# Experts on 32 tiles of 256 tokens and 7 of 128 instead of 39 of 256, with another routing chain and products of zeros beside it

## Chip, cores and metric

The kernel runs on one core of one Trainium2 chip. The metric is the device time of one execution in microseconds, from the first to the last instruction and the little around it; the median of three executions stands for a kernel.

## The reference

The input is one sequence of 4096 tokens with 256 features. Three parts follow one another, each on the layer norm of the residual stream: a mixture of experts (half its output is added), a causal attention with 16 heads, and the same mixture of experts again.

```python
logits = einsum('bsd,de->bse', x, gate_w) + gate_b
probs = softmax(logits, axis=1)                 # over the tokens
vals, idx = top_k(probs, 2)                     # 2 of 8 experts for each token
h = relu(einsum('bsd,edo->ebso', x, w1) + b1)   # three layers of 256 x 256
h = relu(einsum('ebso,eop->ebsp', h, w2) + b2)
y = relu(einsum('ebso,eop->ebsp', h, w3) + b3)
v = einsum('ebso,bse->eo', y, w_tok)            # one row of 256 for each expert
out = einsum('bse,eo->bso', ind, v)             # each token adds its two experts' rows
```

Each expert's outputs are summed over its tokens, each weighted by its probability. Only the tokens that chose an expert count, 8192 pairs of token and expert in all.

## The kernel before, in words

Each mixture of experts ("block" f = 0 and f = 1) has a **routing** and a **stream of tiles**. The 8192 pairs are sorted by expert into slots, and each expert's slots are rounded up to whole tiles of 256: at most 39 tiles, whatever the tokens choose, and the kernel always works on 39.

*Routing* (`route`, lines 1291 to 1435 on VectorE) is one chain on VectorE, in which nearly every step waits for the one before (`prev()`); each step counts up the semaphore `routed`, and `ROUTED[name]` is its place. It picks each token's two experts (to `chosen`, L1345), lets TensorE count tokens for each expert (L978, L979), works out where each expert's tiles start (`counts` to `slots`, L1355 to L1378), gives each pair its slot (to `digits_lo`, L1390), and makes one-hot matrices ("hots", L1396 to L1401: four batches of three instructions) from which 64 matmuls (L989) build the inverse, from slot to token. Between the counts and the hots TensorE transposes the chosen experts for the later combination (L985, eight groups of four matmuls, which ScalarE copies out at L763). From the inverse come the row numbers of each half tile (`code` to `row_no`, L1405 to L1414), then each tile's expert (`tile_cmp` to `tile_mask`) and the matrix that sums tiles to experts (`from_start` to `tile_hot`).

*The stream.* GpSimd gathers a tile's token rows with one indirect DMA for each 128 tokens (`load_tile`, L502), two for a tile, into a ring of three tiles. Then the engines run a software pipeline over j, each in the order that is written out:

- TensorE (`tiles`): third layer of tile j-3, transposes of tile j (L1020, 4), second layer of tile j-2, transposes of its weights (L1027, 2), first layer of tile j-1. A layer (L1009) is 4 products of 128x128 weights with 256 columns in f32; each product is two records in the trace, so a layer has 8 records, and a tile 24 and 6 transposes.
- VectorE (`tiles`): the token weights of tile j (`widen_weight`, L1459 to L1465), bias and weight on the third layer of tile j-3 (`weigh`, L1472), a copy of an expert's layer weights into place (`stage`, L1451, whose expert number is first loaded into a register), bias and relu of the second layer of tile j-2 (`relu_second`, L1481), and two more `stage` copies. The last of the three waits for ScalarE's relu of tile j-1, since it overwrites the bias that this relu reads.
- ScalarE (`tiles`): relu and sum of tile j-3 (L775), the copies of the transposes of tile j (L781, L785), relu of the first layer of tile j-1 (L791).

Activations and staged weights have two buffers each, and each layer has one PSUM bank. After the last tile its sums are transposed (L1042) and combined (L1057) with the residual stream.

## Time and profile before

| what | value |
|---|---|
| median of 3 runs | 2256.11 us (2255.95 to 2260.18) |
| the profiled execution: its own time | 2256.6 us |
| its span | 2254.6 us |
| busy shares: TensorE, VectorE, ScalarE, GpSimd | 95%, 82%, 72%, 23% |
| mean granted TensorE clock | 0.973 |

The profile counts an engine as busy while it executes; loading a register and waiting for a semaphore are not busy time. The granted clock is TensorE's, as a share of 2.4 GHz: 1.00 is 2.4 GHz, 0.50 is 1.2 GHz. Times in the trace are from the start of the span. The stream of block 0 ends at 308.75 us, the attention follows, and block 1 begins its routing at 1960.2 us.

### The profile page before, as it was taken

Reading aid. Unit: us, or ns where it says so; the run is one execution under the profiler, and the core shown is the slowest. Engines: PE = TensorE matmul, PEld = TensorE weight load, DVE = VectorE, ACT = ScalarE, POOL = GpSimd, SP = SyncE. Lnnn points to the kernel's source line nnn. Section 1 sums busy time; section 2 is a strip of 40 time slices with the busy share of each in tenths; the row PEclk is TensorE's granted clock in tenths of the full one; section 3 lists DMA queues with packets and bytes.
Section 4 is the critical chain, followed back from the end, with each engine's and each line's share of the span. In section 5 each row is a group of like instructions: output and inputs, shape, how many; then the busy total and the mean of one; then the engine's idle time right before and its main releaser. Section 6 shows DMA issues by size and latency. Waiting matters only on the chain.

```text
span 2254.6 us, 98008 instructions
## 1 busy us (share of the span) xinstructions
PE 2149.0 (95%) x42449; PEld 1870.9 (83%) x42449; DVE 1850.2 (82%) x3873; ACT 1625.3 (72%) x3556; POOL 528.6 (23%) x1307
## 2 busy tenths in 40 slices
PE   4899988999999999999999999999999999689997
PEld 3788866388999999999999999998999997568885
DVE  7555555899999999999999999999999993765555
ACT  5244445588888888888888888888888887424442
POOL 1333302422121221222212213122122210033330
PEclk8899989999999999999999999999999999879998
DMA  8211203410010110100101001011010002131112
GB/s 262 71 48 47 46 8 102 145 32 17 20 32 4 32 25 11 32 11 25 30 6 32 23 13 32 7 30 25 11 32 12 24 4 93 29 114 48 46 48 81
DMA packets 95527, 96.23 MB, mean 43 GB/s; under 512 B 41332, under 2 KB 84088, under 8 KB 95096
## 3 DMA queue, kind: packets, MB, share of 16 engines
q0 software_dynamic: 42048, 44.80, 7.9%
q1 hardware_dynamic: 52624, 45.15, 6.3%
q8 instruction: 334, 5.47, 1.0%
q14 instruction: 97, 0.79, 0.1%
q10 hardware_dynamic: 424, 0.01, 0.0%
HBM read 64.14 MB, written 25.43 MB: 40 GB/s over the span
## 4 chain that ended last, share of the span: by engine, by line
PE 89%; DVE 4%; issue 3%; ACT 1%; POOL 1%; DMA 1%; SPq 1%; ACTq 0%; POOLq 0%; DVEq 0%
PE bank L1108 43%; PE bank L1100 19%; PE bank L1009 18%; PE bank L1146 2%; PE bank L1020 2%; PE bank L1063 1%; PE bank L1211 1%; PE bank L989 1%; DVE stats L1241 1%; PE bank L1027 1%; PE bank L1154 1%; PE bank L1076 0%; SPq L621 0%; DVE rows L1263 0%; DVE x_res L1514 0%
## 5 line engine op out<-in xcount | busy, mean ns | idle before, releaser
L1108 PE MATMUL bank<-work 96*32 96x512 bf16 (+4 forms) x17920 | 1413.2, 363 | 3.2 <-DVE work L1553 2.8
L842 ACT ACTIVATE feat<-bank 128x512 f32<-128x512 f32 (+3 forms) x2304 | 1251.5, 565 | 153.9 <-PE bank L1108 76.7
L1553 DVE TENSOR_REDUCE work<-bank 128x1 f32<-128x512 f32 (+3 forms) x2176 | 1299.5, 639 | 62.0 <-PE bank L1108 50.3
L1100 PE MATMUL bank<-feat,phase 128*17 128x128 f32 x16896 | 1137.8, 272 | 1.6 <-issue 1.6
L1100 PEld LDWEIGHTS bank<-feat,phase 128*17 128x17 f32 x16896 | 829.5, 98 | 66.9 <-issue 2.5
L1108 PEld LDWEIGHTS bank<-work 96*32 96x32 bf16 (+1 forms) x17920 | 808.1, 96 | 69.3 <-DVE work L1553 11.4
L1009 PE MATMUL bank<-work 128*128 128x256 f32 x1872 | 434.9, 382 | 3.7 <-issue 2.6
L1009 PEld LDWEIGHTS bank<-work 128*128 128x128 f32 x1872 | 340.6, 191 | 53.9 <-issue 12.3
L1451 DVE COPY work<-phase 128x514 f32 x234 | 100.5, 429 | 189.5 <-DVE work L1472 56.4
L560 POOL TENSOR_SCALAR_AFFINE_SELECT feat<-feat 128x128 f32<-128x128 f32 x512 | 147.2, 295 | 444.5 <-ACT feat L842 436.2
L502 POOL DMA_INDIRECT work<-token_table,row_no x156 | 149.2, 956 | 327.6 <-DVE work L1465 242.0
L775 ACT ACTIVATE work<-work 128x256 f32<-128x256 f32 x156 | 63.6, 408 | 180.9 <-DVE work L1472 180.9
L791 ACT ACTIVATE work<-bank,work 128x256 f32<-128x256 f32 x156 | 65.5, 471 | 87.5 <-PE bank L1009 79.3
L567 POOL TENSOR_TENSOR rows<-work 128x64 f32<-128x64 f32 x128 | 37.5, 293 | 330.4 <-DVE work L1564 306.2
L529 POOL DMA_DIRECT2D work<-qk_parts x180 | 107.0, 596 | 5.1 <-PE bank L1108 3.2
L551 POOL CAST work<-work 128x4 bf16<-128x4 f32 x128 | 24.0, 187 | 340.2 <-DVE work L1559 340.2
L1550 DVE TENSOR_REDUCE work<-bank 128x4 f32<-128x512 f32 x128 | 88.0, 688 | 1.6 <-PE bank L1154 1.6
L1146 PE MATMUL bank<-work 96*32 96x128 bf16 (+3 forms) x2048 | 84.4, 201 | 0.8 <-issue 0.8
L1472 DVE SCALAR_TENSOR_TENSOR work<-bank,work 128x256 f32<-128x256 f32 x156 | 67.8, 475 | 11.1 <-PE bank L1009 10.9
L1146 PEld LDWEIGHTS bank<-work 96*32 96x32 bf16 x2048 | 68.7, 95 | 9.8 <-issue 3.3
L781 ACT ACTIVATE work<-bank 128x512 f32<-128x512 f32 x78 | 45.0, 577 | 42.6 <-PE bank L1020 40.7
L1108 PE MATMUL bank<-ident,work 128*32 128x68 f32 x1024 | 70.7, 226 | 0.4 <-ACT work L858 0.4
(175 smaller groups left out, 1414.0 us busy)
## 6 DMA issues: line engine op xcount, KB each, us to landing
phase<-in_w SPq DMA_DIRECT2D x12, 1024.0 KB, 11.7
work<-qk_parts POOLq DMA_DIRECT2D x60, 192.0 KB, 4.2
token_table<-rows SPq DMA_DIRECT2D x8, 1056.0 KB, 9.6
qk_parts<-phase SPq DMA_DIRECT2D x20, 384.0 KB, 2.7
work<-qk_parts POOLq DMA_DIRECT2D x60, 128.0 KB, 4.3
qk_parts<-work SPq DMA_DIRECT2D x12, 384.0 KB, 2.6
x_res<-in_x SPq DMA_DIRECT2D x8, 512.0 KB, 8.8
work<-work SPq DMA_DIRECT2D x256, 1.0 KB
```

The lines of the kernel that those rows point to most:

```text
L502: eng.indirect_dma_start(out=x_slot[:, j % NXG, u, :], out_offset=None, in_=table[f], in_offset=bass.IndirectOffsetOnAxis(ap=row_no[:, n:n ...
L529: eng.dma_start(stack[r * HD:(r + count) * HD, h % 2, c, tokens], src).then_inc(sig.stack[h % 2], 16)
L560: eng.affine_select(out=p_ring[:, n % P_RING, lo:lo + P], in_=p_ring[:, n % P_RING, lo:lo + P], compare_op=ALU.is_ge, fill=0.0, base=0, pa ...
L842: eng.activation(p_ring[:, n % P_RING, lo:QB], s_bank("probs", n)[:, lo:QB], ACT.Exp, scale=HD ** -0.5).then_inc(sig.s_done, 1)
L1009: mm = eng.matmul(bank[bk][:, m * TILE:(m + 1) * TILE], staged[:, b, l, k * D + m * P:k * D + (m + 1) * P], acts[:, l, b, k], start=(k == ...
L1100: mm = eng.matmul(bank[ACC_BANK][GRID * g:GRID * g + VW, 0:P], v_aug[:, t, h, :], p_ring[:, n % P_RING, g * P:(g + 1) * P], start=(t == 0) ...
L1108: mm = eng.matmul(out[GRID * g:GRID * (g + 1), width], left[:, GRID * g:GRID * (g + 1)], right, start=start, stop=stop)
L1146: eng.matmul(tiles[GRID * g:GRID * (g + 1), i, 0:GRID * (g + 1)], stack[0:QK_ROWS, h % 2, 0, q0 + GRID * g:q0 + GRID * (g + 1)], stack[0:Q ...
L1451: eng.tensor_copy(staged[:, j % 2, l, :], experts[:, bass.ds(expert, 1), l, :].rearrange("p a w -> p (a w)"),).then_inc(sig.staged[f], 1)
L1472: eng.scalar_tensor_tensor(weighted[:, j % 2, m], bank[4][:, m * TILE:(m + 1) * TILE], staged[:, j % 2, 2, KD * D + m:KD * D + m + 1], w_r ...
L1550: eng.tensor_reduce(maxima[:, h % 2, j, :, 0], scores[:, 0:QB].rearrange("p (i s) -> p i s", i=TPJ), AX_X, ALU.max).then_inc(sig.a_done, 1)
L1553: eng.tensor_reduce(maxima[:, h % 2, j, i, k + 1:k + 2], scores[:, 0:hi - lo], AX_X, ALU.max).then_inc(sig.a_done, 1)
```

## The change

The stream has 39 tiles as before, but 32 are wide (256 tokens) and 7 narrow (128 tokens, one gather, products of 128 columns, transposes of half the number). `ORDER` puts a narrow tile first, then five or six wide ones before each further narrow one, and a narrow one last. Where an expert's slots don't fill a wide tile, its rest goes into a wide tile while such are left, and else into one or two narrow ones; the routing chain works this out in new steps on small operands (`rounded` to `beyond_by`), several of which don't wait for the one before. `beyond`, `beyond_slots` and `all_slots` are new on full-size operands. In turn `chosen`, `counts`, `prior`, the tile steps, `code`, `row_f` and `row_clamped` go, the counting matmuls take the operand in the order expert, tile, the inverse is 71 columns wide instead of 78, and the steps from `tile_cmp` to `tile_mask` stand before the wait for the inverse instead of behind the row numbers. Four of the eight groups of L985 move behind the 64 matmuls of L989.

TensorE also multiplies zeros by zeros into bank 4, 512 columns in bf16, with no reader (`busy_beside`): one product after each of the 17 steps before `chosen_bf`, one after each of the 9 steps from `row_scaled`, and 5 more behind them, all of the last 14 ahead of the first tile. In the second step of the stream TensorE does the first layer of tile 0 before the transposes of tile 1.

```diff
-MAGIC = 1.5 * 2 ** 30
-N_TILES = (TOP * S + E * (TILE - 1)) // TILE
-N_SUB = N_TILES * TS
+MAGIC, MAGIC_TILE = 1.5 * 2 ** 30, 1.5 * 2 ** 31
+LO_MIDDLE = (P - 1) / 2
+WIDE, NARROW = TOP * S // TILE, E - 1
+N_TILES = WIDE + NARROW
...
+FIRST_CHOSEN, FIRST_ROW = "chosen_bf", "row_scaled"
+GATHER_FILL = 5
+ORDER = [WIDE]
+for _n in range(NARROW - 1):
+    ORDER += [*range(WIDE * _n // (NARROW - 1), WIDE * (_n + 1) // (NARROW - 1)), WIDE + _n + 1]
+SUBS = [[TS * t, TS * t + 1] if t < WIDE else [WIDE * TS + t - WIDE] for t in ORDER]
...
-                for u in range(TS):
-                    n = j * TS + u
+                for u, n in enumerate(SUBS[j]):
                     eng.indirect_dma_start(
                         out=x_slot[:, j % NXG, u, :], out_offset=None, in_=table[f],
...
-                    ).then_inc(sig.slot[f][j % NXG], 16)
+                    ).then_inc(sig.slot[j % NXG][u], 16)
...
+            def chosen_rows(f, m0, m1):
+                need.wait_ge(sig.chosen_wide[f], 1)
+                need.wait_ge(sig.feat[2 * f], KD * NT // 4)
+                for m in range(m0, m1):
+                    need.wait_ge(sig.chosen_copy[f], m - 1)
+                    for i in range(4 * m, 4 * m + 4):
+                        eng.matmul(bank[m % 2][0:V_ROWS, (i - 4 * m) * P:(i - 4 * m + 1) * P], chosen_wide[:, i, :],
+                                   ident_bf[:, :], start=True, stop=True).then_inc(sig.chosen_tr[f], 1)
+            def busy_beside(f, steps):
+                for name in steps:
+                    need.wait_ge(sig.routed[f], ROUTED[name])
+                    eng.matmul(bank[4][:, :], zeros_bf[:, 0:P], zeros_bf[:, :], start=True, stop=True)
             def route(f):
-                flat = chosen_bf[:, :, :].rearrange("p i e -> p (i e)")
...
+                if f == 1:
+                    need.wait_ge(sig.attended, NT // 2)
+                busy_beside(f, ROUTE[:ROUTE.index(FIRST_CHOSEN)])
...
-                eng.matmul(bank[5][:, 0:NT * E], before[:, :], flat, start=True, stop=True).then_inc(sig.counted[f], 1)
-                eng.matmul(bank[6][:, 0:NT * E], ones_bf[:, :], flat, start=True, stop=True).then_inc(sig.counted[f], 1)
...
+                eng.matmul(bank[5][:, 0:NT * E], not_before[:, :], by_expert, start=True, stop=True).then_inc(sig.counted[f], 1)
+                eng.matmul(bank[6][:, 0:NT * E], ones_bf[:, :], by_expert, start=True, stop=True).then_inc(sig.counted[f], 1)
...
                                start=(b == 0), stop=(b == TOP * NT - 1)).then_inc(sig.inverse[f], 1)
+                chosen_rows(f, NT // 8, NT // 4)
...
+                busy_beside(f, ROUTE[ROUTE.index(FIRST_ROW):])
+                busy_beside(f, ROUTE[-1:] * GATHER_FILL)
                 for j in range(N_TILES + LAYERS):
                     layer(f, j - 3, 2)
+                    if j == 1:
+                        layer(f, j - 1, 0)
                     if j < N_TILES:
                         transpose_tile(f, j)
                     layer(f, j - 2, 1)
                     if j < N_TILES:
                         transpose_weight(f, j)
-                    layer(f, j - 1, 0)
+                    if j != 1:
+                        layer(f, j - 1, 0)
                 need.wait_ge(sig.v_part[f], KD * N_TILES)
...
-                step("chosen", eng.tensor_tensor(chosen[:, :, :], sel[:, 0], sel[:, 1], ALU.add))
...
-                step("chosen_bf", eng.tensor_copy(chosen_bf[:, :, :], chosen[:, :, :]))
...
+                step("chosen_bf", eng.tensor_tensor(chosen_bf[:, :, :], sel[:, 0], sel[:, 1], ALU.add))
+                prev()
+                step("weights", eng.tensor_tensor(rows[:, :, D:ROW], chosen_bf[:, :, :], probs[:, :, :], ALU.mult))
...
                 need.wait_ge(sig.counted[f], 2)
                 prev()
-                step("counts", eng.tensor_copy(em, bank[6][:, 0:NT * E].rearrange("p (i e) -> p e i", e=E)))
...
-                step("running", eng.tensor_tensor_scan(flat_run, carry[:, :, :].rearrange("p e i -> p (e i)"), flat_em,
...
-                step("prior", eng.tensor_tensor(prior, run, em, ALU.subtract))
...
-                step("steps_gt", eng.tensor_tensor(steps_gt[:, :, :], run[:, :, NT - 1:NT].to_broadcast(SE),
...
-                step("tiles_of", eng.tensor_reduce(pe_col(5), steps_gt[:, :, :], AX_X, ALU.add))
...
-                step("tile_end", eng.tensor_tensor_scan(pe_col(6), ones_e[:, :], pe_col(5), 0.0, ALU.mult, ALU.add))
...
-                step("tile_start", eng.tensor_tensor(pe_col(7), pe_col(6), pe_col(5), ALU.subtract))
...
-                step("slot_start", eng.tensor_scalar(pe_col(8), pe_col(7), float(TILE), None, ALU.mult))
...
+                step("running", eng.tensor_tensor_scan(flat_run, carry[:, :, :].rearrange("p e i -> p (e i)"),
+                                                       bank[6][:, 0:NT * E], 0.0, ALU.mult, ALU.add))
+                prev()
+                total, full, rest = run[:, :, NT - 1], pe_col(5), pe_col(9)
+                full_sum, left = small[:, 6, 0:1], small[:, 6, 1:2]
+                step("rounded", eng.tensor_scalar(full, total, (1 - TILE) / 2, MAGIC_TILE, ALU.add, ALU.add))
...
+                step("full", eng.tensor_scalar(full, full, MAGIC_TILE, None, ALU.subtract))
...
+                step("expert_rest", eng.tensor_tensor(rest, total, full, ALU.subtract))
+                step("full_sum", eng.tensor_reduce(full_sum, full, AX_X, ALU.add))
+                prev()
...
+                step("over_half", eng.tensor_scalar(over_half, rest, P + 0.5, None, ALU.is_gt))
+                step("left", eng.tensor_scalar(left, full_sum, -1.0 / TILE, float(WIDE), ALU.mult, ALU.add))
...
+                step("others", eng.scalar_tensor_tensor(others, rest, 0.5, over_half, ALU.is_gt, ALU.subtract))
...
+                prev()
+                step("rank", eng.tensor_tensor_scan(rank, ones_e[:, :], rests, 0.0, ALU.mult, ALU.add))
+                prev()
+                step("in_wide", eng.scalar_tensor_tensor(in_wide, rank, left, rests, ALU.is_le, ALU.mult))
...
+                step("wide_some", eng.scalar_tensor_tensor(wide_some, pe_col(14), float(TILE), full, ALU.mult, ALU.add))
+                step("not_in_wide", eng.tensor_tensor(narrow_of, rests, in_wide, ALU.subtract))
...
+                step("wide_slots", eng.scalar_tensor_tensor(wide_slots, pe_col(15), float(TILE), wide_some, ALU.mult,
+                                                            ALU.add))
+                step("narrow", eng.scalar_tensor_tensor(narrow, pe_col(16), 2.0, pe_col(17), ALU.mult, ALU.add))
...
+                step("wide_end", eng.tensor_tensor_scan(wide_end, ones_e[:, 0:E], wide_slots, 0.0, ALU.mult, ALU.add))
+                step("narrow_sum", eng.tensor_tensor_scan(pe_col(12), ones_e[:, 0:E], narrow, 0.0, ALU.mult, ALU.add))
...
+                step("slot_start", eng.scalar_tensor_tensor(pe_col(8), wide_end, -LO_MIDDLE, wide_slots, ALU.add,
+                                                            ALU.subtract))
+                step("narrow_end", eng.tensor_scalar(narrow_end, pe_col(12), float(P), float(NARROW_0), ALU.mult, ALU.add))
...
+                step("narrow_start", eng.scalar_tensor_tensor(narrow_start, narrow, -float(P), narrow_end, ALU.mult,
+                                                              ALU.add))
+                prev()
+                step("beyond_by", eng.tensor_tensor(beyond_by, narrow_start, wide_end, ALU.subtract))
                 step("position", eng.tensor_tensor(
-                    scratch[:, 3], bank[5][:, 0:NT * E].rearrange("p (i e) -> p i e", e=E),
-                    prior.rearrange("p e i -> p i e"), ALU.add))
...
+                    by_expert(slots), bank[5][:, 0:NT * E].rearrange("p (e i) -> p e i", e=E), run, ALU.add))
...
+                step("beyond", eng.tensor_tensor(beyond, slots, bc(wide_slots, 1, PNE), ALU.is_ge))
...
+                step("beyond_slots", eng.tensor_tensor(beyond, beyond, bc(beyond_by, 1, PNE), ALU.mult))
+                step("slots", eng.tensor_tensor(slots, slots, bc(pe_col(8), 1, PNE), ALU.add))
...
+                step("all_slots", eng.tensor_tensor(slots, slots, beyond, ALU.add))
...
-                step("rounded", eng.tensor_scalar(rounded, slot, 0.5 - P / 2, MAGIC, ALU.add, ALU.add))
...
-                step("digits_hi", eng.tensor_scalar(hi, rounded, MAGIC, None, ALU.subtract))
...
-                step("digits_lo", eng.tensor_tensor(lo, slot, hi, ALU.subtract))
+                step("digits_hi", eng.tensor_scalar(hi, slot, MAGIC, MAGIC, ALU.add, ALU.subtract))
...
+                step("digits_lo", eng.scalar_tensor_tensor(lo, slot, LO_MIDDLE, hi, ALU.add, ALU.subtract))
...
-                need.wait_ge(sig.inverse[f], TOP * NT)
...
-                step("code", eng.tensor_copy(code[:, :], bank[7][:, 0:N_SUB]))
...
-                step("row_f", eng.tensor_copy(row_no_f[:, :], code[:, :].bitcast(I32)))
...
-                step("row_clamped", eng.tensor_scalar(row_no_f[:, :], row_no_f[:, :], 0.0, None, ALU.max))
...
+                step("tile_cmp", eng.tensor_tensor(tile_cmp[:, 0:WIDE, :], bc(tile_slots[:, 0:WIDE], 2, WIDE_E),
...
+                step("narrow_cmp", eng.tensor_tensor(tile_cmp[:, WIDE:N_TILES, :],
...
                 prev()
                 step("tile_mask", eng.tensor_tensor(tile_mask[:, :, :], bc(tile_exp[:, :], 2, TE),
...
+                need.wait_ge(sig.inverse[f], TOP * NT)
+                prev()
+                step("row_scaled", eng.tensor_scalar(row_no_f[:, :], bank[7][:, 0:N_SUB].bitcast(I32), 2.0 ** -16,
+                                                     1.0 - CODE_0, ALU.mult, ALU.add))
+                prev()
+                step("row_no", eng.tensor_scalar(row_no[:, :], row_no_f[:, :], 0.0, None, ALU.max))
...
+                step("first_slot", eng.tensor_tensor(pe_col(7), wide_end, wide_slots, ALU.subtract))
...
+                step("tile_slot", eng.tensor_tensor(slot, tile_col[:, :], narrow_col[:, :], ALU.min))
...
+                step("from_start", eng.tensor_scalar(tile_hot[:, 0, :], pe_col(7), slot, None, ALU.is_le))
+                step("from_end", eng.tensor_scalar(tile_hot[:, 1, :], wide_end, slot, None, ALU.is_le))
...
+                step("start_by", eng.scalar_tensor_tensor(tile_hot[:, 0, :], narrow_start, slot, tile_hot[:, 0, :],
...
+                step("end_by", eng.scalar_tensor_tensor(tile_hot[:, 1, :], narrow_end, slot, tile_hot[:, 1, :],
...
+                need.wait_ge(sig.chosen_tr[f], NT)
+                eng.tensor_tensor(w_pick[:, b, 0:n], x_slot[:, j % NXG, 0:n, D:ROW],
+                                  bc(tile_mask[:, ORDER[j], :], 1, [P, n, E]), ALU.mult).then_inc(sig.w_col[f], 1)
...
+                need.wait_ge(sig.w_tr[f], subs_before(j - 1))
+                eng.tensor_copy(w_wide[:, b, 0:n], bc(w_col[:, b, 0:n], 2, [P, n, P])).then_inc(sig.w_col[f], 1)
...
-                        weighted[:, j % 2, m], bank[4][:, m * TILE:(m + 1) * TILE],
...
+                        weighted[:, j % 2, m, 0:WIDTH[j]], bank[4][:, m * TILE:m * TILE + WIDTH[j]],
...
-                    eng.tensor_scalar(acts[:, 2, j % 2, m], bank[3][:, m * TILE:(m + 1) * TILE],
+                    eng.tensor_scalar(acts[:, 2, j % 2, m, 0:WIDTH[j]], bank[3][:, m * TILE:m * TILE + WIDTH[j]],
```

The same narrowing by `WIDTH[j]` stands in ScalarE's instructions and in `layer`, and the loops over the halves of a tile run over `SUBS[j]`.

## Rows read from the trace of the kernel before

**Rows 1.** The chain that ended last, shares of the span by line.

```profile
PE bank L1108 43%; PE bank L1100 19%; PE bank L1009 18%; PE bank L1146 2%; PE bank L1020 2%; PE bank L1063 1%; PE bank L1211 1%; PE bank L989 1%; DVE stats L1241 1%; PE bank L1027 1%; PE bank L1154 1%; PE bank L1076 0%; SPq L621 0%; DVE rows L1263 0%; DVE x_res L1514 0%
```

**Rows 2.** Windows: length, busy of PE, PEld, DVE, ACT, POOL; clock, DMA, GB/s.

```profile
38.00:55.00 17.00, 5.13 (x34) 3.69 (x34) 14.98 (x35) 10.11 (x12) 0.41 (x1) 0.50 0.60 203
55.00:65.00 10.00, 9.59 (x61) 8.55 (x62) 8.07 (x10) 0.00 (x0) 0.00 (x0) 0.50 0.53 167
76.00:80.00 4.00, 3.42 (x13) 2.57 (x13) 0.43 (x1) 1.24 (x4) 3.08 (x4) 0.71 0.42 113
86.00:299.00 213.00, 212.71 (x1086) 182.85 (x1085) 123.12 (x362) 91.12 (x292) 62.53 (x66) 1.00 0.17 43
```

**Rows 3.** Timeline of one tile of block 1: start, us, instruction, [idle before <-releaser].

```profile
2033.60 0.60 PE L1020 MATMUL bank<-ident,work 128*128 128x128 f32 x4
2034.04 1.89 PE L1009 MATMUL bank<-work 128*128 128x256 f32 x8
2034.09 0.17 DVE L1459 TENSOR_TENSOR work<-work,feat 128x16 f32<-128x16 f32 x1
...
2035.98 3.64 PE L1009 MATMUL bank<-work 128*128 128x256 f32 x16
...
2036.69 0.87 DVE L1481 TENSOR_SCALAR work<-bank,work 128x256 f32<-128x256 f32 x2
...
2037.91 0.84 ACT L791 ACTIVATE work<-bank,work 128x256 f32<-128x256 f32 x2 [1.03 <-PE bank L1009]
...
2039.59 0.43 DVE L1451 COPY work<-phase 128x514 f32 x1 [0.84 <-ACT work L791]
...
2039.94 0.17 DVE L1459 TENSOR_TENSOR work<-work,feat 128x16 f32<-128x16 f32 x1
```

**Rows 4.** Timeline of VectorE, a tile of block 0 that it began late.

```profile
197.57 0.17 DVE L1459 TENSOR_TENSOR work<-work,feat 128x16 f32<-128x16 f32 x1
...
202.71 0.43 DVE L1451 COPY work<-phase 128x514 f32 x1 [0.47 <-issue]
203.05 0.17 DVE L1459 TENSOR_TENSOR work<-work,feat 128x16 f32<-128x16 f32 x1
```

**Rows 5.** Timeline of the weight loads of L933, whose matmuls have 32 columns.

```profile
1957.44 0.53 PEld L933 LDWEIGHTS bank<-ident,v_rest 128*128 128x128 f32 x4
```

**Rows 6.** Timeline of block 0, from the chosen experts to the first tiles.

```profile
45.54 0.29 DVE L1347 CAST chosen_bf<-feat 128x256 bf16<-128x256 f32 x1
...
46.54 0.42 DVE L1355 COPY feat<-bank 128x256 f32<-128x256 f32 x1 [0.24 <-PE bank L979]
...
52.45 1.15 PE L985 MATMUL bank<-ident_bf,work 128*96 128x128 bf16 x8 [0.20 <-ACT feat L763]
52.69 0.81 DVE L1396 TENSOR_TENSOR work<-work,digits 128x1248 bf16<-128x1248 bf16 x1
...
65.75 0.24 DVE L1405 COPY code<-bank 128x78 f32<-128x78 f32 x1 [2.69 <-PE bank L989]
...
66.74 0.20 DVE L1414 CAST row_no<-row_no_f 128x78 uint32<-128x78 f32 x1
...
67.25 1.37 POOL L502 DMA_INDIRECT work<-token_table,row_no  x1 [28.00 <-DVE row_no L1414]
...
68.93 1.04 POOL L502 DMA_INDIRECT work<-token_table,row_no  x1 [0.30 <-issue]
...
71.80 1.11 PE L1020 MATMUL bank<-ident,work 128*128 128x128 f32 x4 [6.08 <-DMA work<-token_table,row_no]
...
79.92 1.97 PE L1009 MATMUL bank<-work 128*128 128x256 f32 x8 [0.58 <-issue]
```

**Rows 7.** Timeline of block 0, the last tiles of the stream.

```profile
293.73 10.53 PE L1009 MATMUL bank<-work 128*128 128x256 f32 x48
...
305.27 1.96 PE L1009 MATMUL bank<-work 128*128 128x256 f32 x8 [1.01 <-issue]
...
308.75 0.41 PE L1042 MATMUL bank<-ident,v_part 128*39 128x128 f32 x2 [1.52 <-ACT work L775]
```

More of the change, by code:

```diff
@@ L190, in attention_steps, with subs_before, slot_uses @@
         yield "divide", u
+def subs_before(j):
+    return sum(len(subs) for subs in SUBS[:max(j, 0)])
+def slot_uses(f, j, u):
+    fills = [n for n in range(j % NXG, N_TILES, NXG) if u < len(SUBS[n])]
+    return f * len(fills) + sum(n <= j for n in fills)
 class Waits:
@@ L753, in route @@
                 widen_ids(f)
[L754 removed]
+                need.wait_ge(sig.routed[f], ROUTED["chosen_bf"])
                 if f == 1:
@@ L1344, in route @@
                 prev()
-                step("chosen", eng.tensor_tensor(chosen[:, :, :], sel[:, 0], sel[:, 1], ALU.add))
+                step("chosen_bf", eng.tensor_tensor(chosen_bf[:, :, :], sel[:, 0], sel[:, 1], ALU.add))
                 prev()
-                step("chosen_bf", eng.tensor_copy(chosen_bf[:, :, :], chosen[:, :, :]))
-                prev()
-                step("weights", eng.tensor_tensor(rows[:, :, D:ROW], chosen[:, :, :], probs[:, :, :], ALU.mult))
-                flat_em, flat_run, flat_prior = (scratch[:, n].rearrange("p i e -> p (i e)") for n in range(3))
```

140 lines of the change are left out of this document (68 added, 72 removed).

## The prediction

> **What bounds the kernel now.** I read the chain of waits first: it names what the end of the span hangs on. By line, nearly all of it is matmuls. L1108 and L1100, 62% of the span, belong to the attention, which the change doesn't touch; L1009, the layers of the expert tiles, holds 18%, and the transposes of the tiles (L1020, L1027) 3% [rows 1]. So the two streams of tiles, some 450 us together, run at TensorE's pace. The windows say the same: from 86 to 299 us TensorE is busy 212.71 of 213.00 us at a granted clock of 1.00. In the routing before it the clock is 0.50: there VectorE is the busy engine, and TensorE works little from 38 to 55 us, then 96% of the time from 55 to 65 us on matmuls of 78 columns without the clock rising; it rises only between 76 and 80 us, once the wide products run [rows 2].
>
> The timeline of one tile tells how much room the other engines have, and that decides what half a tile is worth. From one start of L1459 to the next is 5.85 us [rows 3]. *TensorE:* from the transposes to the second layer are 0.44 us, 0.11 for each of four; from that layer to the next are 1.94 us, which is 8 records and 2 transposes, so 0.216 us a record; 24 x 0.216 + 6 x 0.11 = 5.84 us, so it is never idle. *VectorE:* its busy time alone misleads (123 of 213 us), since loading an expert number is not counted. Its one wait is for ScalarE's relu, which ends at 2037.91 + 0.84 = 2038.75, in front of the last copy; the copy has 0.84 us of non-busy time before it. In a tile that VectorE began late, that time is 0.47 us, and the tile takes 203.05 - 197.57 = 5.48 us [rows 4]. So VectorE needs 5.48 us a tile: 0.37 us of room, no more.
>
> **The narrow tile on TensorE.** A record of 128 columns streams half as long, 0.108 us. Its weights are still 128x128 in f32. The four loads of L933, whose own matmuls are too short to hide them, take 0.53 us end to end, at most 0.13 each [rows 5], and the transposes, with the same load and 128 columns, are 0.11 us apart [rows 3]. Lower end 0.11, upper 0.13; I take 0.11, the row with the same column count. A narrow tile is 24 x 0.11 + 3 x 0.11 = 2.97 us, 2.87 less than a wide one; at 0.13 it is 3.45. The saving is spread: 0.33 us in the step j in which the tile is transposed, 0.85 in each of the next three (its first, second and third layer).
>
> A load that isn't hidden would turn this round. The Trainium skill ("TensorE: Matmul & The Clock Gate", Part 3) says that a weight load overlaps matmuls in flight only when its row group differs, and there ("LDWEIGHTS") that it takes columns / 1.2 GHz, 107 ns here. By that a wide record would be 0.107 + 0.213 = 0.32 us; the rows have 0.216, so the trace disagrees.
>
> **The narrow tile on VectorE.** A full-size copy of 256 columns takes 0.42 us [rows 6] and one of 16 takes 0.17 [rows 3]: 0.13 us for each 128 columns. `weigh` and `relu_second` have two such instructions each, so 0.27 + 0.27 us less, and `widen_weight` about 0.07. The three staged copies of 514 columns and their register loads stay. So over the four steps that a narrow tile touches, VectorE needs 5.41, 5.48, 5.21, 5.21 us and TensorE 5.51, 4.99, 4.99, 4.99. The larger of each: 5.51 + 5.48 + 5.21 + 5.21 = 21.41, against 4 x 5.85 = 23.40: **2.0 us** saved, not 2.87. That is the upper end, because the engines also hang together. The second relu ends at 2036.69 + 0.87 = 2037.56, and the third layer wants it 8 records after 2035.98, at 2037.71 [rows 3]: 0.15 us ahead. Once VectorE sets the pace TensorE waits there and the next wide tile pays some back. If every step stays tied to this ring (room 0.1 us a step, ScalarE's relu 0.3 shorter, VectorE 0.6 shorter), the narrow tile gives 4 x 0.1 + 0.9 = **1.3 us**. I take 1.7, between the two. Five narrow tiles lie amid wide ones: 5 x 1.7 = **8.5 us** a block.
>
> **The last narrow tile** has nothing behind it. The last 48 records run from 293.73, the last layer from 305.27, the sums' transpose at 308.75 [rows 7]. Three layers 0.87 shorter and three transposes less: 2.9; two relus, two weighings and ScalarE's sums shorter: 0.4; less 0.5, as tile 37's second relu (0.9 us, begun 0.4 us after its layer) isn't done when the shorter layer of tile 38 is. **2.8 us** a block.
>
> **The routing chain.** A small step with a wait costs 0.2 us, a full-size one 0.45 (with the gap to the next) [rows 3, 6]. Removed: the cast 0.32, `counts` 0.45, `prior` 0.46, the five tile steps 1.2, one rounding 0.2, `code`, `row_f`, `row_clamped` 0.7, and 7 of 78 columns of eight hot instructions of 0.81, 0.56: 3.9 us. Added: 12 small steps with a wait, 2.4; 7 without, 0.1 each, 0.7; three full-size ones, 1.3: 4.4 us. The moved `tile_cmp` to `tile_mask` (2.2 us) hide under the 2.69 us in which VectorE waits for L989 [rows 6]; uncovered they would cost 2.2. Net **+0.5 us**: row numbers at 67.4 instead of 66.9.
>
> **The zeros and the first tile.** The 17 early products follow steps 0.45 us apart. At 1.2 GHz 512 columns take 0.43, so they keep up and the counting matmuls wait for nothing. The 14 late ones sit ahead of the first tile. L989 now ends 1.2 us later, at 66.9; the four moved groups take 2 x 1.15 [rows 6], to 69.2. Then 14 products: at 2.4 GHz 0.21 each, 3.0 us, to 72.2; at 1.2 GHz 6.0 us, to 75.2. I expect 1.2 GHz at first, as it was there before [rows 2], and a rise on the way, since the products leave no gap: the first transposes at 74.0, against 71.80. The gather isn't late by then: two issues at 67.25 and 68.93 brought the data 2.9 us after the second; one issue brings it at about 70.9. So the stream starts 2.2 us later, but closer packed: narrow layers of tile 0, all the ring's gathers landed, clock at 1.00. From 74.0: transposes and their copy 0.8, first layer 0.9, transposes of tile 1 0.5, their copies and the relu on ScalarE 1.7, then VectorE's stage 1.1 and weights of tile 2 0.7, transposes 0.2: tile 1's first layer at 79.9. Before, it followed the second layer of tile 0 (79.92 + 1.73) and two transposes: 82.0. So 2.1 us sooner, and 0.3 more for tile 0's third layer: **2.4 us** a block. Ends: 1.2 us less with 1.2 GHz throughout, 1.9 more if nothing held the first tile.
>
> **Sum.** A block: 2.4 + 8.5 + 2.8 = 13.7; both 27.4. The profiled execution is 2256.6 (span 2254.6), 0.5 above the median of 2256.11. 2256.6 - 27.4 = 2229.2; **2229.0**.
>
> **Rivals.**
> *A, TensorE sets the pace in narrow tiles too*, if VectorE's room in the wide ones can be spent on the narrow: 32 x 5.48 + 7 x 4.87 = 209.5 us of VectorE against 32 x 5.84 + 7 x 2.97 = 207.7 of TensorE, nearly even. 5 x 2.87: block 19.6, time 2217.5. Against it: two buffers, and the 0.15 us at the second relu.
> *B, VectorE has no room*, the 0.47 and 0.84 being the same work in another order: 0.6 us for each of the five, block 8.2, time 2240. The short tile speaks against it [rows 4].
> *C, loads not hidden at 128 columns*: records of 0.22, so TensorE saves only transposes; block 2, time 2252.6: no change. This is what the rule cited above would make of the change; the 0.11 of the transposes speaks against it.
> *D, slower: narrow layers let the clock fall.* Place: the three steps after each narrow tile, where TensorE now waits. TensorE has been 96% busy with short matmuls at 0.50 [rows 2]. One tile at 1.2 GHz costs 5.8 us more; a fall at each of six narrow tiles gives 6 x 5.8 = 35 a block against 13.7 saved: 2299. It decides from 2.4 falls a block. Against it: even then TensorE works 4.99 of 5.48 us.
>
> **How the numbers follow.** My forecast (2222 to 2236) 0.72, A 0.08, B 0.12, C 0.03, D 0.05. Its own bounds: 5 x 1.3 and the late start, 1.2 + 6.5 + 2.8 = 10.5 a block, 2236; 5 x 2.0 and the early one, 4.3 + 10.0 + 2.8 = 17.1, 2222. The range reaches to A and B: 2217 to 2241. A measurement can tell some 0.2%, 4.5 us. Faster 0.92, same 0.03, slower 0.05.
>
> **What would show it.** Right: a narrow tile's layer in 0.9 us, its records 0.11 apart; steps of about 5.5, 5.5, 5.25, 5.25 us around it, with TensorE idle there before L1009 and VectorE's wait for ScalarE gone; first transposes near 74; L1042 some 13.7 us earlier in block 0. Wrong: records of 0.13 or more; a granted clock of 0.50 inside the stream; products still running after 76; an attention of another length.

## The result, and the profile after

The changed kernel takes 2231.16 us, the median of 4 runs (2229.80 to 2234.71); the kernel before took 2256.03 in 4 runs beside it. The ratio is 0.989, 95% interval 0.9877 to 0.9903: 25 us, faster. The forecast was 2229.0 us, range 2217 to 2241.

The profiled execution of the changed kernel took 2234.71 us (span 2232.9), the slowest of its four, against 2256.6 of the profiled one before; so the two profiles differ by 21.9 us. The windows of the changed kernel, in the columns of [rows 2]:

```profile
38.00:55.00 17.00, 10.17 (x33) 3.32 (x33) 14.16 (x46) 8.06 (x8) 0.41 (x1) 0.60 0.60 208
55.00:65.00 10.00, 7.21 (x49) 6.35 (x50) 10.00 (x13) 0.00 (x0) 0.00 (x0) 0.50 0.51 160
70.00:74.00 4.00, 3.70 (x16) 1.57 (x14) 2.24 (x7) 0.51 (x3) 3.09 (x4) 0.87 0.43 109
86.00:280.00 194.00, 188.78 (x1005) 161.79 (x1004) 114.32 (x343) 82.16 (x272) 56.16 (x59) 1.00 0.16 43
```

The stream runs at a granted clock of 1.00 throughout, and TensorE, which had 0.29 us without work in 213 [rows 2], now has 5.2 us in 194. The true loss is larger, since the profile models the ends of matmuls and a record's tail covers the start of a wait: by the pace of the records 27 wide and 5 narrow tiles want 27 x 5.84 + 5 x 2.97 = 172.5 us, and the 32 steps that hold them take 181.87 (next table). The clock is at 1.00 before the first tile (0.87 from 70 to 74 us), where it rose only between 76 and 80 before.

To see where the time went I mark each block at four records of the timeline: VectorE's first of the routing, the start of VectorE's token weights of tile 6 (L1459, now L1546), that of tile 38's, and the product that follows the sums' transpose. Block 0 of the changed kernel: 35.79, 100.95, 282.82, 298.10 us; of the kernel before: 35.59, 103.49, 291.56, 309.67. In us, block 0 / block 1:

| part | before | changed | gained | forecast |
|---|---|---|---|---|
| routing and first six tiles | 67.90 / 68.07 | 65.16 / 65.82 | 2.7 / 2.3 | 2.4 |
| 32 steps, five narrow tiles | 188.07 / 188.29 | 181.87 / 181.75 | 6.2 / 6.5 | 8.5 |
| last tiles and sums | 18.11 / 17.86 | 15.28 / 15.28 | 2.8 / 2.6 | 2.8 |
| block | 274.08 / 274.21 | 262.31 / 262.85 | 11.8 / 11.4 | 13.7 |

The two blocks gave 23.1 us; the attention between them was 1.2 us longer in this profile (1651.69 against 1650.49). That says nothing of the change: in the fourteen profiles of this document the attention takes 1646.9 to 1653.9 us. A narrow tile amid wide ones is worth 6.2 / 5 = 1.24 us in one block and 1.31 in the other, not 1.7.

The routing of block 0, in the timeline of the changed kernel, as [rows 6]:

```profile
45.29 0.42 DVE L1391 TENSOR_TENSOR chosen_bf<-feat 128x256 bf16<-128x256 f32 x1
...
45.77 0.61 PE L1024 MATMUL bank<-chosen_bf,not_before 128*128 128x256 bf16 x1
46.21 0.63 PE L1025 MATMUL bank<-chosen_bf,ones_bf 128*128 128x256 bf16 x1
46.87 0.69 DVE L1401 TENSOR_TENSOR_SCAN feat<-carry,bank 128x256 f32<-128x256 f32 x1 [0.70 <-PE bank L1025]
...
54.95 0.75 DVE L1474 TENSOR_TENSOR work<-work,digits 128x1136 bf16<-128x1136 bf16 x1
...
67.62 0.20 DVE L1502 TENSOR_SCALAR row_no<-row_no_f 128x71 uint32<-128x71 f32 x1
...
69.79 3.59 PE L1011 MATMUL bank<-zeros_bf 128*128 128x512 bf16 x13 [0.22 <-issue]
...
73.21 0.38 PE L1061 MATMUL bank<-ident,work 128*128 128x128 f32 x2
...
78.06 0.44 PE L1061 MATMUL bank<-ident,work 128*128 128x128 f32 x2 [1.15 <-DMA work<-token_table,row_no]
...
79.50 2.67 PE L1050 MATMUL bank<-work 128*128 128x256 f32 x15
```

The row numbers are ready at 67.82 us, 0.9 after those of before (66.94); 0.2 of it is that the routing itself began 0.2 us later, so 0.7 against a forecast of 0.5. The last of the late products of zeros starts at 73.0, and the first transposes follow at 73.21 (forecast 74.0).

The two counting matmuls, which now read their operand in the order expert, tile, start 0.44 us apart. In the kernel before, they started 0.19 us apart at half the granted clock:

```profile
45.89 0.40 PE L978 MATMUL bank<-chosen_bf,before 128*128 128x256 bf16 x1 [10.34 <-DVE chosen_bf L1347]
46.08 0.42 PE L979 MATMUL bank<-chosen_bf,ones_bf 128*128 128x256 bf16 x1
```

So VectorE waits 0.70 us for them instead of 0.24 [rows 6]. The products of zeros are not the cause: without them (no_products, below) the two start 0.43 us apart and VectorE waits 0.79 us.

Three steps round a narrow tile, whose first layer is the record of 108.64, in the timeline of the same kernel:

```profile
108.64 1.06 PE L1050 MATMUL bank<-work 128*128 128x128 f32 x8
108.76 0.43 DVE L1535 COPY work<-phase 128x514 f32 x1 [0.77 <-DVE work L1559]
...
109.11 0.87 DVE L1568 TENSOR_SCALAR work<-bank,work 128x256 f32<-128x256 f32 x2
...
110.08 1.97 PE L1050 MATMUL bank<-work 128*128 128x256 f32 x8 [0.38 <-issue]
110.74 0.43 DVE L1535 COPY work<-phase 128x514 f32 x1 [0.77 <-DVE work L1568]
111.58 0.43 DVE L1535 COPY work<-phase 128x514 f32 x1 [0.40 <-issue]
...
111.92 0.17 DVE L1546 TENSOR_TENSOR work<-work,feat 128x16 f32<-128x16 f32 x1
...
115.36 0.84 ACT L817 ACTIVATE work<-bank,work 128x256 f32<-128x256 f32 x2 [0.64 <-PE bank L1050]
...
117.03 0.43 DVE L1535 COPY work<-phase 128x514 f32 x1 [0.69 <-issue]
117.37 0.17 DVE L1546 TENSOR_TENSOR work<-work,feat 128x16 f32<-128x16 f32 x1
...
120.90 1.97 PE L1050 MATMUL bank<-work 128*128 128x256 f32 x8 [0.43 <-issue]
...
122.76 0.17 DVE L1546 TENSOR_TENSOR work<-work,feat 128x16 f32<-128x16 f32 x1
```

The narrow layer takes 1.06 us, its eight records some 0.11 apart, as forecast; so no weight load shows. TensorE then waits 0.38 us, until 110.08: the second relu ended at 109.11 + 0.87 = 109.98. VectorE is idle in these steps only ahead of its copies, mostly for 0.77 or 0.40 us (a finished semaphore and a register load), and its steps take 5.45 and 5.39 us. One of these gaps, the 0.69 us ahead of 117.03, still hangs on ScalarE: its relu ended at 115.36 + 0.84 = 116.20, and the copy follows 0.83 us later, as it did before (0.84 [rows 3]). Ahead of the other last copies that wait is gone, and VectorE is what TensorE waits for.

The last tiles of block 0, as [rows 7]:

```profile
284.39 6.50 PE L1050 MATMUL bank<-work 128*128 128x256 f32 x32
...
291.28 2.85 PE L1050 MATMUL bank<-work 128*128 128x256 f32 x16 [0.39 <-issue]
...
294.88 1.13 PE L1050 MATMUL bank<-work 128*128 128x128 f32 x8 [0.75 <-DVE work L1568]
...
297.18 0.41 PE L1088 MATMUL bank<-ident,v_part 128*39 128x128 f32 x2 [1.17 <-ACT work L801]
```

The sums' transpose starts 308.75 - 297.18 = 11.6 us earlier than before.

### The profile page after: what moved, and what is told of

The parts are those of the page before. It is cut to its first block, busy times and chain, and to the rows that moved or that the text cites. A ratio compares the mean times of both kernels' runs of the same rounds, so it can differ in the third digit from the quotient of the medians.

```text
span 2232.9 us, 98125 instructions
## 1 busy us (share of the span) xinstructions
PE 2135.2 (96%) x42465; PEld 1845.8 (83%) x42469; DVE 1846.4 (83%) x3903; ACT 1615.7 (72%) x3556; POOL 513.2 (23%) x1295
## 4 chain that ended last, share of the span: by engine, by line
PE 88%; DVE 5%; issue 3%; ACT 1%; POOL 1%; DMA 1%; SPq 1%; DVEq 0%; ACTq 0%; POOLq 0%
PE bank L1154 44%; PE bank L1146 19%; PE bank L1050 17%; PE bank L1192 2%; PE bank L1061 1%; PE bank L1109 1%; PE bank L1257 1%; DVE stats L1287 1%; PE bank L1068 1%; PE bank L1200 1%; PE bank L1122 1%; SPq L646 0%; DVE rows L1309 0%; DVE x_res L1601 0%; DVE work L1476 0%
## 5 line engine op out<-in xcount | busy, mean ns | idle before, releaser
L1050 PE MATMUL bank<-work 128*128 128x256 f32 (+1 forms) x1872 | 404.4, 363 | 14.2 <-issue 10.9
L1050 PEld LDWEIGHTS bank<-work 128*128 128x128 f32 x1872 | 319.1, 190 | 63.0 <-issue 19.3
L527 POOL DMA_INDIRECT work<-token_table,row_no x142 | 135.5, 954 | 320.7 <-DVE work L1552 241.7
L801 ACT ACTIVATE work<-work 128x256 f32<-128x256 f32 (+1 forms) x156 | 60.6, 389 | 183.8 <-DVE work L1559 183.8
L817 ACT ACTIVATE work<-bank,work 128x256 f32<-128x256 f32 (+1 forms) x156 | 62.5, 452 | 69.3 <-PE bank L1050 69.3
L1192 PE MATMUL bank<-work 96*32 96x64 bf16 (+3 forms) x2048 | 84.3, 201 | 0.0
L1559 DVE SCALAR_TENSOR_TENSOR work<-bank,work 128x256 f32<-128x256 f32 (+1 forms) x156 | 64.1, 452 | 8.6 <-PE bank L1050 8.6
L1568 DVE TENSOR_SCALAR work<-bank,work 128x256 f32<-128x256 f32 (+1 forms) x156 | 64.0, 452 | 0.0
## 6 DMA issues: line engine op xcount, KB each, us to landing
phase<-in_w SPq DMA_DIRECT2D x12, 1024.0 KB, 11.8
```

Source lines behind the costliest of these rows:

```text
L527: eng.indirect_dma_start(out=x_slot[:, j % NXG, u, :], out_offset=None, in_=table[f], in_offset=bass.IndirectOffsetOnAxis(ap=row_no[:, n:n ...
L1050: mm = eng.matmul(bank[bk][:, m * TILE:m * TILE + WIDTH[j]], staged[:, b, l, k * D + m * P:k * D + (m + 1) * P], acts[:, l, b, k, 0:WIDTH[j]],
L1192: eng.matmul(tiles[GRID * g:GRID * (g + 1), i, 0:GRID * (g + 1)], stack[0:QK_ROWS, h % 2, 0, q0 + GRID * g:q0 + GRID * (g + 1)], stack[0:Q ...
L1559: eng.scalar_tensor_tensor(weighted[:, j % 2, m, 0:WIDTH[j]], bank[4][:, m * TILE:m * TILE + WIDTH[j]], staged[:, j % 2, 2, KD * D + m:KD ...
```

## The experiments

Three sets of four, each set on one chip with the kernel before beside it (medians of before: 2256.09, 2257.37 and 2259.70 us). Ratios are to those runs.

| kernel | median, us | ratio (95%) | 32 steps, us |
|---|---|---|---|
| *first set* no_products | 2235.24 | 0.9909 (0.9896 to 0.9923) | 181.89 |
| padded | 2254.69 | 0.9996 (0.9987 to 1.0005) | 188.49 |
| own_step | 2217.90 | 0.9830 (0.9816 to 0.9843) | 176.08 |
| fixed_expert | 2210.36 | 0.9802 (0.9789 to 0.9816) | 173.42 |
| *second set* after_again | 2239.20 | 0.9913 (0.9894 to 0.9931) | 181.86 |
| own_before | 2253.98 | 0.9984 (0.9974 to 0.9995) | 187.04 |
| own_no_products | 2229.58 | 0.9864 (0.9841 to 0.9886) | 176.07 |
| own_relu_early | 2218.95 | 0.9825 (0.9805 to 0.9844) | 172.97 |
| *third set* own_step_2 | 2226.57 | 0.9859 (0.9837 to 0.9881) | 176.09 |
| own_relu_2 | 2219.91 | 0.9836 (0.9813 to 0.9860) | 172.96 |
| own_relu_no_early | 2220.99 | 0.9838 (0.9816 to 0.9860) | 172.96 |
| own_relu_none | 2218.84 | 0.9828 (0.9803 to 0.9852) | 172.97 |

The last column is the middle part of block 0 as in the table above. For one kernel it repeats to 0.02 us between chips (in block 1 to 0.1), so it says more than the medians, which for one kernel differ by 8 or 9 us between sets.

**padded: is it the narrowness at all?** The routing, the order and the products stay; a narrow tile gets a second half that gathers the zero row.

```diff
-SUBS = [... if t < WIDE else [WIDE * TS + t - WIDE] for t in ORDER]
+SUBS = [... if t < WIDE else [WIDE * TS + t - WIDE, N_SUB] for t in ORDER]
...
-        row_no = sb("row_no", [P, N_SUB], U32)
+        row_no = sb("row_no", [P, N_SUB + 1], U32)
...
+            const(eng.memset(row_no[:, N_SUB:N_SUB + 1], 0))
```

> The changed kernel with its 7 narrow tiles done at the full width of 256: their second half gathers the zero row, so that the output is the same; the routing, the order and the products stay. Theory: the narrow tiles gave 1.24 us in the middle of the stream and 2.83 us at its end, so 2 x (5 x 1.24 + 2.83) = 18 us is lost and the time is 2249 us; the start of the stream stands as in the changed kernel, the last tile ends 9 us later in each block. Rival (the gain came from the routing, the clock and the order, and the narrowness gives only its drain): 2237 us.

2254.69 us: next to nothing is left of the gain. The middle part is 188.49 us, that of before, and the last one 17.86. The start part is 67.30 / 66.64, so about 1.5 of the 2.5 us gained there came from the narrow first tile too (the mean of 2.1 and 0.8, from one profile). A block is only 0.4 and 1.4 us shorter than before, so all the rest is the narrowness; I had expected the loss 6 us smaller.

**no_products: the products of zeros.**

```diff
-                busy_beside(f, ROUTE[:ROUTE.index(FIRST_CHOSEN)])
...
-                busy_beside(f, ROUTE[ROUTE.index(FIRST_ROW):])
-                busy_beside(f, ROUTE[-1:] * GATHER_FILL)
```

> The changed kernel without its 62 products of zeros (17 before the routing's choice, 14 after it, in each block); all else as it is. If the products after the routing give what the prediction put on them (the clock up before the first transposes), the start of the tile stream comes later in each block by 1 to 3 us, the clock stands at 0.50 until some us after the first transposes as it did before the change, and the time is 2233 to 2238 us. If they do nothing and the start was gained by the shorter chain and the moved copies of the choice alone, 2231 us within 1. If they stand in the way (they run for 3.6 us just before the first transposes), 2228 to 2230 us.

The median lies 4 us above 2231.16, but was taken in another set than that one. In the profile the start part is 65.27 / 65.39 us, against 65.16 / 65.82 with them. This profile's routing began 0.76 us later. Counted from there, the clock rises 5.1 us later (at 76.89, instead of 71.03), but the first transposes come 1.6 us sooner, since no products stand ahead of them (at 72.37, instead of 73.21). The one pays for the other in this profile.

**own_step: the ring through the last copy.** `stage` of the first layer does tile j at the end of step j, no longer tile j+1, whose buffer ScalarE's first relu of the same step still reads.

```diff
                     stage(f, j, 1)
-                    stage(f, j + 1, 0)
+                    if j:
+                        stage(f, j, 0)
```

The list `STAGES`, by which TensorE counts the copies, is changed to match.

> VectorE copies the first layer's weights of tile j at the end of step j, and no longer those of tile j+1, so that the copy does not wait for ScalarE's first ReLU of the same step. Theory (the ring through that copy paces the steps round a narrow tile): the wait of the last copy for ScalarE is gone, a narrow tile in the middle is worth 1.9 us and not 1.24, and the time is 2224 us, 2218 to 2228. Rival 1 (VectorE's own work with its register loads paces those steps): 2231 us within 1.5, the narrow tile still 1.2 to 1.4. Rival 2 (TensorE's weight loads pace a narrow layer): 2231 us, and TensorE's own records show no wait between the layers.

2217.90 us, 13 us below the changed kernel: twice what the theory gave. The middle part is 176.08 us, so a narrow tile is worth (188.07 - 176.08) / 5 = 2.40 us instead of 1.24. The start part is shorter too, by 1.5 and 3.6 us, and the last part 0.9 us longer in each block. The timeline shows the third layer of the wide tile that follows a narrow one:

```profile
119.63 1.59 PEld L1050 LDWEIGHTS bank<-work 128*128 128x128 f32 x8 [0.51 <-DVE work L1568]
120.35 0.43 DVE L1535 COPY work<-phase 128x514 f32 x1 [0.77 <-DVE work L1568]
121.19 0.43 DVE L1535 COPY work<-phase 128x514 f32 x1 [0.41 <-issue]
```

TensorE's weight loads still wait 0.51 us for the second relu there.

**fixed_expert: no register loads.** Each copy takes an expert known when the kernel is built, so it computes other experts' layers.

```diff
-                expert = eng.value_load(tile_exp_i[0:1, t:t + 1], min_val=0, max_val=E - 1)
...
-                                experts[:, bass.ds(expert, 1), l, :].rearrange("p a w -> p (a w)"),
+                                experts[:, t % E:t % E + 1, l, :].rearrange("p a w -> p (a w)"),
```

> Each copy of weights takes an expert known at compile time, so VectorE loads no register and copies from a fixed place; what it computes is another expert's product, the work is the same. Theory (VectorE's step, ring or work, is what holds the narrow tiles): without the register load each copy comes 0.3 to 0.6 us sooner, the narrow tile is worth 2.3 to 2.87 us, and the time is 2215 us, 2212 to 2221. Rival (TensorE's weight loads or its queue pace the narrow layers): 2230 us within 2.

2210.36 us, 2 us below the range that I gave; a narrow tile is worth (188.07 - 173.42) / 5 = 2.93 us, TensorE's full 2.87 within 0.1. The window says so, and the timeline shows VectorE waiting for ScalarE again, 1.55 us ahead of its last copy, though the ring is in place:

```profile
90.00:270.00 180.00, 180.00 (x981) 159.44 (x980) 113.45 (x331) 82.12 (x267) 56.23 (x59) 1.00 0.17 45
```

```profile
118.21 0.43 DVE L1534 COPY work<-phase 128x514 f32<-128x514 f32 x1
119.24 0.84 ACT L817 ACTIVATE work<-bank,work 128x256 f32<-128x256 f32 x2 [1.28 <-PE bank L1050]
120.18 0.43 DVE L1534 COPY work<-phase 128x514 f32<-128x514 f32 x1 [1.55 <-ACT work L817]
```

So TensorE's loads and its queue are out as causes: it does narrow tiles at full pace when VectorE is ready.

**own_before: is the moved copy faster in itself?** The edit of own_step in the kernel before.

> The kernel before the change with the copy of the first layer's weights moved to the step's own tile, as in own_step. Theory (the ring costs nothing while every step is TensorE's 5.84 us, it costs only where narrow layers leave TensorE less): 2256 us within 2, and a tile still takes 5.85 us. Rival (the moved copy is faster in itself, narrow or not): 2243 us, the 13 us that own_step gained.

Ratio 0.9984: 3.4 us by the medians. The middle parts are 1.0 and 1.4 us shorter, where the same edit gave 5.8 and 5.6 in the changed kernel. Without narrow tiles TensorE sets the step and the ring costs little. It also shows that part of own_step's gain has nothing to do with narrow tiles: against this kernel a narrow tile of own_step is worth (187.04 - 176.08) / 5 = 2.19 us.

**own_relu_early: the order on VectorE.** own_step, and:

```diff
+                    if 0 <= j - 2 < N_TILES:
+                        relu_second(f, j - 2)
                     stage(f, j - 1, 2)
-                    if 0 <= j - 2 < N_TILES:
-                        relu_second(f, j - 2)
```

> own_step, and VectorE does the second ReLU of tile j-2 ahead of the copy of the third layer's weights of tile j-1, and no longer behind it. In own_step a middle narrow tile was worth 2.40 us, and TensorE waited for the second ReLU round it (0.51 us in the step of a narrow first layer). Theory: that wait is what is left of the 2.87; the narrow tile is now worth 2.8 us and the time is 2214 us, 2212 to 2216. Rival (VectorE's sum of work is full in those steps, the order of it doesn't matter): 2218 us within 1.5, the narrow tile still 2.4.

The middle part is 172.97 us, within 0.5 of the 172.5 us that TensorE alone wants, and TensorE's records show no idle time in it. A narrow tile is worth 3.0 us against the kernel before, 2.8 against own_before. The time, 2218.95 us, is 3 us above the range that I gave and by itself would fit the rival; but own_step had not run on this chip. So I measured the same kernel again, with own_step beside it:

> own_relu_early once more. Its middle part was 173.0 and 173.3 us, 3 us a block below own_step, but its profile had the late signals in both blocks. On the same chip as own_step_2: theory, 5 to 6 us less than own_step_2. Rival (the earlier second ReLU brings the stop about, or costs as much elsewhere): the same as own_step_2 within 2 us.

> own_step once more, beside the three that follow. The profiles of one kernel agree to 0.3 us in the middle of the stream (181.87 and 181.86 us for 32 tiles in the two of the changed kernel) and differ by 2 to 3 us in the routing with the first six tiles, where in some profiles TensorE's signals come 2 to 5 us late and the clock falls again. Middle part 176.1 us; time 2218 us without such a stop, 2223 to 2227 with one in each block.

2219.91 against 2226.57 us: 6.7 us, where the theory had 5 to 6. In the two profiles the blocks are 4.8 us shorter, 3.1 and 2.8 of it in the middle parts and 1.1 given back in the other parts; the attention, which is the same code in both, is 3.9 us shorter. The window of own_relu_2, and its timeline in a step with a narrow second layer:

```profile
90.00:270.00 180.00, 180.00 (x981) 159.58 (x980) 112.23 (x333) 82.25 (x266) 55.72 (x59) 1.00 0.17 45
```

```profile
113.55 0.17 DVE L1546 TENSOR_TENSOR work<-work,feat 128x16 f32<-128x16 f32 x1
...
115.80 0.43 DVE L1535 COPY work<-phase 128x514 f32 x1 [0.17 <-issue]
116.57 0.43 DVE L1535 COPY work<-phase 128x514 f32 x1 [0.34 <-issue]
...
117.40 0.43 DVE L1535 COPY work<-phase 128x514 f32 x1 [0.41 <-PE bank L1050]
...
117.75 0.17 DVE L1546 TENSOR_TENSOR work<-work,feat 128x16 f32<-128x16 f32 x1
```

VectorE does the same instructions in 117.75 - 113.55 = 4.20 us, where the changed kernel needed 5.4. The time ahead of two of the copies fell from 0.77 to 0.17 and 0.34. In the old order the first two copies each wait, by the code, for the instruction just ahead (the third layer's for `weigh`, the second layer's for `relu_second`, which free the buffers), so that the register load starts only when that one has ended; now other work stands between. The third gap fell from 0.69 us, behind ScalarE's relu, to 0.41. Together that is 1.3 us, the whole difference.

**after_again, and what the chips differ in.**

> The changed kernel itself once more, beside the kernel before in the same rounds: 2231 us, 2229 to 2234, and a ratio of 0.989. It says how far two medians of one kernel lie apart, which bounds what the runs without products can show.

2239.20 us, 8 above the first measurement and 5 above the range that I gave. The middle and last parts are the same to 0.1 us; the start part is 67.92 / 67.88 us instead of 65.16 / 65.82. These 4.8 us are what the profiles show of the 8; where the rest lies isn't shown. The timeline of after_again:

```profile
75.48 0.60 PE L1061 MATMUL bank<-ident,work 128*128 128x128 f32 x4
...
78.02 0.60 ACT L806 ACTIVATE work<-bank 128x512 f32<-128x512 f32 x1 [3.48 <-remote]
78.25 0.94 POOL L527 DMA_INDIRECT work<-token_table,row_no  x1 [1.39 <-remote]
...
78.67 1.09 PE L1061 MATMUL bank<-ident,work 128*128 128x128 f32 x4 [2.37 <-ACT work L806]
```

ScalarE and GpSimd both wait for those transposes, recorded as done at 76.08; both go on about 2 us later, and "remote" means that the trace has no record that released them. TensorE is then without work, and the clock falls again, as the windows of after_again show:

```profile
76.00:78.00 2.00, 0.29 (x3) 0.06 (x1) 0.05 (x1) 0.00 (x0) 0.86 (x1) 1.00 0.48 120
78.00:80.00 2.00, 1.33 (x6) 1.17 (x7) 0.00 (x0) 1.59 (x5) 1.44 (x2) 0.68 0.10 32
80.00:82.00 2.00, 2.00 (x11) 1.94 (x11) 1.23 (x5) 0.39 (x1) 0.44 (x1) 0.50 0.43 104
82.00:84.00 2.00, 2.00 (x12) 1.78 (x11) 1.15 (x4) 0.46 (x2) 1.63 (x2) 0.96 0.22 51
```

All eight profiles of the second and third sets have such a late signal at the start of the stream, in both blocks; none of the four of the first set has, nor has the changed kernel's first profile. The clock falls again after it in at least one block of seven of the eight, but not in own_before. The kernel before has one too in the profile that the gains are counted from, in block 0 alone:

```profile
78.74 0.60 PE L1020 MATMUL bank<-ident,work 128*128 128x128 f32 x4
...
81.64 0.60 ACT L781 ACTIVATE work<-bank 128x512 f32<-128x512 f32 x1 [1.86 <-remote]
```

It cost that profile next to nothing: TensorE's first layer of tile 0 [rows 6] streams until 79.92 + 1.73 = 81.65 us, and its next matmul starts at 81.72.

**The products once more.**

> own_step without the 62 products of zeros. The profile of no_products had the same length from the first routing step to the sums as the changed kernel (262.4 against 262.3 and 262.9 us), but its median was 4 us above. If the products are worth nothing: 2218 us within 2. If they are worth the 4 us: 2222 us.

> own_relu_early without the 17 products of zeros per block that stand ahead of the counting matmuls; the 14 late ones stay. The early ones raised the clock for 3.4 us and it fell again long before the tiles, so theory: the same as own_relu_2 within 1.5 us. Rival (they matter for the start of the stream): 3 to 10 us above own_relu_2.

> own_relu_early with no product of zeros at all. If the late products do what they are there for, the clock rises 4 us later in each block and the time is 3 to 10 us above own_relu_2 (no_products lay 4 us above the changed kernel on one chip, own_no_products 11 us above own_step, but on two chips). If they do nothing: the same as own_relu_2 within 1.5 us.

On the chip of the third set the three kernels with all, some and none of the products take 2219.91, 2220.99 and 2218.84 us, with runs from 2214 to 2227: no difference that the runs can show. own_no_products, at 2229.58, lay above both of the times that I had given; it is 3 us above own_step_2 and 12 above own_step, neither of them on its chip, so by itself it says little. The profiles leave one sign for the products: in the two kernels of these chips that have none, the stop in block 0 is longest. VectorE waits 5.1 us in own_no_products and 6.5 in own_relu_none, whose start part is 70.19 us there against 66.70 in own_relu_2, but 65.78 against 65.87 in block 1. Whether the products cause that isn't shown. With five runs a kernel that scatter over up to 10 us, a worth of a few us either way isn't excluded.

## Why the prediction was right, and where it was off

**The bound and the narrow tile on TensorE: right.** Records of 0.11 us, nothing added for the loads, and a tile worth 2.87 us to TensorE alone; fixed_expert (2.93) and own_relu_early (3.0, or 2.8 against own_before) gave it in full. Rivals C and D are out, and B (0.6 us a tile) gave half of what was measured: padded put the whole stream back to 188.49 us, and the clock stayed at 1.00. As for the rule of the Trainium skill ("TensorE: Matmul & The Clock Gate", Part 3) that would have made C, the narrow records, 0.11 us apart, disagree with it as the wide ones did. The same part of the page also says that a load may be pulled ahead of matmuls in flight when it goes to the background weight buffer; the prediction left that out. The 0.11 us fit it, though no run here shows such a buffer by itself.

**The narrow tile in the stream: the term that was mis-sized.** The prediction bounded it by 1.3 us (every step tied to the ring) and 2.0 (the larger of the two engines) and took 1.7. It is 1.24 and 1.31: the lower bound. Ten times 0.43 us are the 4.3 us by which this term was too large. The mechanism was named rightly: VectorE becomes what TensorE waits for at the second relu, and its last copy keeps it from working ahead in the wide steps. That the lower bound hit the number is in part luck, for the steps came otherwise. The forecast had some 5.5, 5.5, 5.25 and 5.25 us; VectorE's steps round the narrow tile 12 are 5.54, 5.42, 5.45 and 5.39, then a fifth of 6.27. What I didn't see is that "the larger of the two engines" can't happen with this ring: in a wide step VectorE ends waiting for ScalarE, so it enters each narrow tile with no lead, and the step in which TensorE has wide layers again pays 0.4 us back. own_step takes the ring away and gives 1.16 us more a tile. Its 2.40 us also lie above the 2.0 that the prediction called the upper end: as I read it, a lead lets VectorE meet its need over several steps and not in each.

**Rival A** (2217.5 us) was set aside because of "two buffers, and the 0.15 us at the second relu". It needed no buffer: two copies put elsewhere in VectorE's order brought its middle part about, at 2218.95 and 2219.91 us. The 5.48 us that I read as VectorE's need for a tile [rows 4] was in part not its work but its order: 4.20 us did for a step with one narrow relu, which is 0.27 us shorter than a wide one, so some 4.5 do for a wide step.

**The last tile: right** (2.8 forecast; 2.8 and 2.6).

**The start: right in sum** (2.4 forecast; 2.7 and 2.3), with its parts shifted. The row numbers came 0.4 us later than forecast (0.2 of it a later start), the first transposes 0.8 sooner, since the clock rose early in the late products, at 71.03 us. The first layer of tile 1 starts at 79.50 us (forecast 79.9; 81.99 before). Two readings were wrong. The counting matmuls were given no term for their new order of reading, and VectorE waits 0.46 us longer for them. And "all the ring's gathers landed" is not so: at 78.06 us TensorE had waited 1.15 us for the second half of tile 2. The clock already up, which I put beside the gain as a reason, is not borne out: in no_products the start takes as long. padded shows the narrow first tile as the larger part.

**The median** of 2231.16 lies 2.2 us from the forecast. The blocks gave 4.3 us less than forecast, by the profiles; but the profiled execution was also 3.5 us above that median, so part of the nearness is luck. On another chip the same kernel took 2239.20 us, still inside the range, for a reason that the prediction did not have.

**A version that beats both**: own_relu_early, at a ratio of 0.9825 and 0.9836 to the kernel before in two sets, where the changed kernel has 0.989 and 0.9913. Over own_step its lead is shown on one chip alone (0.9859 there); on the first chip, where no profile has the late signals, own_step had 0.9830.

## What to carry to other kernels

When a change makes the bounding engine's steps shorter, the next engine's need per step decides, and that need is read wrongly from a kernel in which it has time: part of it is the order of its instructions. Look for instructions that wait for the one just ahead of them (here a register load and copy behind the relu that frees the buffer), and for a wait at the end of a step on something that the same step made: it costs nothing while the steps are equal, and keeps the engine from building a lead when they are not. Split the profile at records that mark the phases: here one part repeated to 0.02 us between chips while the medians moved by 8.

## What was not expected of the hardware

A copy from a place given by a register costs VectorE more than its 0.43 us: 0.77 us without other work stand ahead of it when it waits for the instruction before, some 0.40 when it doesn't, and 0.17 to 0.34 in own_relu_2, where other work stands between. fixed_expert has no such gap ahead of its copies, save where it waits for ScalarE. Each of the 39 tiles has three of them.

A matmul of 256 bf16 columns took 0.43 to 0.44 us from start to start when it read its operand in the order expert, tile, at a granted clock of 1.00 and of 0.50 alike; read straight through it took 0.19 us at 0.50.

TensorE's results come some 2 us late once at the start of the stream on two chips and not on the first set's, in every kernel that was profiled there, with and without the products; one profile of the kernel before has it as well. In own_no_products VectorE waits 5.1 us, in own_relu_none 6.5. What holds TensorE is open: its own records show nothing, and no run here was made to find it.
